# A two-layer recurrent block on one core: the next tile is normed channel by channel, B's rows go through memory, and the first round is reordered

## The reference, cut to what matters

```python
xn = _layernorm(x, axis=-1)
s = _L0_attn_ref(xn, ...)        # token-shift mixes, then the recurrence S = decay * S + k v^T
g = _silu(_L0_ffn_ref(xn, ...))  # gated, the two largest of every four hidden units are kept
x = x + s * g
xn = _layernorm(x, axis=-1)
s = _L1_attn_ref(xn, ...)        # 8 "heads" of 512 positions, chunked scan with B, C, X and decays
g = _silu(_L1_ffn_ref(xn, ...))
x = x + s * g
# inside _L1_attn_ref, a state per chunk:
states = jnp.einsum('znj,znjd,znjh->zndh', decay_states, Bc, Xc)
```

## Time and profile before

| | us |
|---|---|
| median of 3 runs (lowest, highest) | 761.48 (760.66, 761.60) |
| the profiled execution: its own time | 761.46 |
| its span in the profile | 759.7 |
| PE busy | 733.9 (97% of the span) |
| DVE busy | 505.5 (67%) |
| ACT busy | 326.0 (43%) |
| POOL busy | 76.6 (10%) |

### The profile page before, as it was taken

One profiled execution on the slowest core, in us unless ns is written; L12 is line 12 of the kernel. 1 busy time (PEld: TensorE's weight loads), 2 busy tenths in 40 slices (PEclk: granted clock), 3 DMA queues, 4 the chain that ended last, 5 costly groups with the idle time before them and its releaser, 6 DMA issues.

```text
span 759.7 us, 18508 instructions
## 1 busy us (share of the span) xinstructions
PE 733.9 (97%) x7316; PEld 601.5 (79%) x7316; DVE 505.5 (67%) x1177; ACT 326.0 (43%) x659; POOL 76.6 (10%) x85
## 2 busy tenths in 40 slices
PE   5897999999999999999999999999999999999997
PEld 3775778877888788886888868888788878888686
DVE  3886578736797367955778467884679736796143
ACT  1322575226632466214752157512664236631570
POOL 6201011101011011000110001100011101101020
PEclk9999999999999999999999999999999999999999
DMA  8800410005000150002400032001500014000320
GB/s 284 330 16 0 127 30 3 1 30 154 2 3 1 48 135 2 3 2 71 113 2 2 3 126 57 3 1 30 149 8 2 1 45 140 2 3 1 99 55 16
DMA packets 33938, 39.77 MB, mean 52 GB/s; under 512 B 20352, under 2 KB 27968, under 8 KB 32192
## 3 DMA queue, kind: packets, MB, share of 16 engines
q1 hardware_dynamic: 33856, 38.49, 16.9%
HBM read 32.12 MB, written 6.36 MB: 51 GB/s over the span
## 4 chain that ended last, share of the span: by engine, by line
PE 93%; DVE 4%; issue 1%; ACT 1%; DMA 0%; POOL 0%; DVEq 0%; SPq 0%; ACTq 0%; POOLq 0%
PE psum L1276 70%; PE psum L1378 4%; PE psum L1488 2%; PE psum L1473 2%; PE psum L1338 2%; PE psum L1349 1%; PE psum L1499 1%; PE psum L1707 1%; PE psum L1526 1%; PE psum L1304 1%; PE psum L1324 1%; PE psum L1361 1%; PE psum L1434 1%; PE psum L1634 1%; PE psum L1441 1%
## 5 line engine op out<-in xcount | busy, mean ns | idle before, releaser
L519 ACT ACTIVATE BC<-psum 64x256 f32<-64x256 f32 x128 | 81.2, 634 | 3.5 <-PE psum L1276 1.8
L1276 PE MATMUL psum<-xnT,sb_f_gate 128*128 128x256 f32 x248 | 62.6, 396 | 1.0 <-ACT xnT L532 0.8
L1276 PE MATMUL psum<-xn1T,sb_n_gate 128*128 128x256 f32 x256 | 61.4, 383 | 0.0
L1276 PE MATMUL psum<-xn1T,sb_n_up 128*128 128x256 f32 x256 | 60.5, 379 | 0.0
L1276 PE MATMUL psum<-xnT,sb_f_up 128*128 128x256 f32 x240 | 58.3, 385 | 0.0
L1276 PEld LDWEIGHTS psum<-xnT,sb_f_gate 128*128 128x128 f32 x248 | 46.2, 194 | 9.9 <-issue 1.7
L1276 PEld LDWEIGHTS psum<-xn1T,sb_n_up 128*128 128x128 f32 x256 | 48.6, 190 | 6.6
L1276 PEld LDWEIGHTS psum<-xn1T,sb_n_gate 128*128 128x128 f32 x256 | 47.3, 190 | 6.5
L867 DVE TENSOR_TENSOR kT<-kT,dec 128x256 f32<-128x256 f32 x56 | 25.7, 458 | 36.0 <-PE psum L1378 29.0
L1276 PE MATMUL psum<-sb_n_down,hidB 128*128 128x256 f32 x224 | 49.5, 379 | 0.0
L1276 PE MATMUL psum<-sb_f_down,hid 128*128 128x256 f32 x224 | 49.5, 379 | 0.0
(11 more groups left out here) (209 smaller groups left out, 1517.1 us busy)
## 6 DMA issues: line engine op xcount, KB each, us to landing
cs_row<-cs_dram SPq DMA_DIRECT2D x8, 1024.0 KB, 5.5
x_dram<-gate SPq DMA_DIRECT2D x8, 512.0 KB, 2.8
cs_half<-cs_dram SPq DMA_DIRECT2D x16, 256.0 KB, 6.4
hidB<-x_dram SPq DMA_DIRECT2D x8, 512.0 KB, 8.1
X<-in_x SPq DMA_DIRECT2D x9, 256.0 KB, 2.7
x<-in_x SPq DMA_DIRECT2D x8, 256.0 KB, 4.1
out_tokens<-thFB SPq DMA_DIRECT2D x8, 256.0 KB, 2.2
sb_w_rkvgo<-in_w_rkvgo SPq DMA_DIRECT2D x1, 1280.0 KB, 5.9
```

The lines of the kernel that those rows point to most:

```text
L519: ins = a_.activation(cols[:, par, 2 * pair:2 * pair + 2, :], src[64 * par:64 * par + 64, :, s, :], ACT.Identity)
L1276: ins = t_.matmul(ps(t, name)[first_row:first_row + rows, col:col + n], w, x, start=(k == 0), stop=(k == len(ws) - 1))
```

## The change

- The next tile is no longer normed by tokens and turned. A second copy of x is laid out on the host with channels on partitions (`x_turned`), and SP loads a tile of it (`XT`, 256 KB) with `X`. DVE's mean and POOL's result go into `token_stats` (128 x 2 x 2). SP stores that (2 KB) and loads it back to every partition (`rows`, 256 KB): step `token_rows`. `next_normed` then is two operations of 128x512 on `XT` (subtract, multiply) that write `xnT`, with the small carry of L975 between. `next_turned` on PE and `next_copied` on ACT are gone. Only tile 0 is still turned on PE.
- `cs16` and its transpose are gone. SP loads `cs_pos` (128 x 16, one float at a time) instead, behind `cs_row`, and POOL waits for `cs_row` alone. `end_args` moves forward on DVE to behind `level_step(2)`.
- `turned_B` is gone. DVE turns B in blocks of 32x32 into `B_turned` (two operations of 128x512, behind `level_step(2)` and `level_step(3)`), SP stores it in `b_dram` with four DMAs, in runs of 32 floats, and loads it back as `Brow` in runs of 64 floats, and `B_decayed` scales it in place. `states` waits for `B_ready`.
- On DVE some of the `sparse_*` steps move back to make room, and `decayed_scores(2)` moves ahead of `hidden_p(3)`. On ACT `end_exp` and the exponentials `L_exps` of layer 1 move forward, `sums_exp` behind them.
- First round: `rank_mix` stands between two halves of the gate product, `mixes` ahead of the up product, the decay weights are a group of their own ahead of the second pair of gate and up weights, and the projection weights follow. `next_normed` stands behind `states_0`.

The core of the diff:

```diff
+            def channels(tile):
+                return A["x_turned"][bass.ds(tile * P, P), :].rearrange("p (h t) -> p h t", h=CH)
+
+            def token_rows(a):
+                wait(rstd_ready, a.count(3, 2))
+                wait(rows_loaded, a.count(16, 16))
+                sp_.dma_start(A["row_dram"].rearrange("(q p two) -> p q two", q=NQ, p=P),
+                              token_stats[:, :, :]).then_inc(rows_stored, 16)
+                wait(rows_stored, a.count(16, 16))
+                sp_.dma_start(rows[:, :, :].rearrange("p t two -> p (t two)"),
+                              A["row_dram"].partition_broadcast(P)).then_inc(rows_loaded, 16)
...
-                    sp_.dma_start(cs16[:, :], cs_dram.rearrange("(c p) -> c p", p=P)).then_inc(cs_loaded, 16)
-                    sp_.dma_start(flat(cs_row), cs_dram.partition_broadcast(P)).then_inc(cs_loaded, 16)
+                    sp_.dma_start(flat(cs_row), cs_dram.partition_broadcast(P)).then_inc(cs_rows_loaded, 16)
+                    sp_.dma_start(cs_pos[:, :], cs_dram.rearrange("(c p) -> p c", p=P),
+                                  allow_slow_non_contiguous=True).then_inc(cs_loaded, 16)
...
+                    if a:
+                        token_rows(a)
+                    wait(B_rows, b.count(16, 16))
+                    wait(B_blocks, b.count(2, 2))
+                    to = b_dram.rearrange("(s n i e d) -> s e i n d", s=NQ, i=32, e=2, d=32)
+                    for s in range(NQ):
+                        for e in range(2):
+                            r = 64 * s + 32 * e
+                            sp_.dma_start(to[s, e], B_turned[r:r + 32, :].rearrange("p (n d) -> p n d", d=32)).then_inc(
+                                B_stored, 16)
+                    wait(B_stored, b.count(64, 64))
+                    sp_.dma_start(Brow.rearrange("p q c d -> p (q c) d"),
+                                  b_dram.rearrange("(c p d) -> p c d", p=P, d=SD)).then_inc(B_rows, 16)
...
-                    norm_apply(X, xn, a.count(3, 2), xn_ready)
-
-                    d.tensor_scalar(xnT[:, :, 0:1], xnT[:, :, T:T + 1], keep[:, bass.ds(a.next().at(), 1)], None,
-                                    ALU.mult).then_inc(carry_ready, 1)
+                    dve.wait_ge(rows_loaded, a.count(16, 32))
+                    dve.wait_ge(xT_loaded, a.count(16, 16))
+                    did(d.tensor_tensor(XT[:, :, :], XT[:, :, :], rows[:, :, 0].unsqueeze(1).to_broadcast([P, CH, T]),
+                                        ALU.subtract))
+                    did(d.tensor_scalar(xnT[:, :, 0:1], xnT[:, :, T:T + 1], keep[:, bass.ds(a.next().at(), 1)], None,
+                                        ALU.mult))
+                    after()
+                    d.tensor_tensor(xnT[:, :, 1:T + 1], XT[:, :, :], rows[:, :, 1].unsqueeze(1).to_broadcast([P, CH, T]),
+                                    ALU.mult).then_inc(xn_ready, 1)
...
+                def B_by_block(half):
+                    wait_freed(dve, b, "B0")
+                    dve.sem_inc(passed, 1)
+                    wait_freed(dve, b, "B1")
+                    n = slice(half * SEQ_T * SH // 2, (half + 1) * SEQ_T * SH // 2)
+                    d.transpose(B_turned[:, n], BC[:, 0, :, :].rearrange("p t h -> p (t h)")[:, n]).then_inc(B_blocks, 1)
...
                     level_step(a, 2)
+                    end_args()
+                    B_by_block(0)
+                    level_step(a, 3)
+                    B_by_block(1)
+                    level_step(a, 4)
                     sparse_compare(a, 0, 1)
                     sparse_compare(a, 0, 2)
-                    level_step(a, 3)
-                    sparse_sums()
-                    level_step(a, 4)
-                    sparse_rest()
                     level_step(a, 5)
                     gate_0()
                     last_update(a)
                     res_gate(0)
                     res_gate(1)
-                    end_args()
+                    sparse_count()
                     hidden_p(a, 2)
                     states_0()
                     B_decayed()
                     decayed_scores(0)
+                    decayed_scores(2)
                     hidden_p(a, 3)
-                    decayed_scores(2)
```

162 lines of the change are left out of this document (81 added, 81 removed), and 2 rows, old and new, of the table FILLS.

## The result

The changed kernel takes 759.57 us (median of 20 runs, 756.5 to 762.22), the kernel before beside it 761.10. The ratio is 0.9963, with a 95% interval from 0.9950 to 0.9976: faster by 0.37%, 2.8 us (the two medians themselves lie 1.5 apart). I had forecast 753.1, a gain of 8.4, three times what the ratio gives. The sign was right and the time lies in the range, but the median is 6.5 us above the forecast. The profiled execution has a time of its own of 760.17 and a span of 758.4.

The account below looks back on a forecast made before the run. PE's list was taken to bound the seven two-layer rounds. Span 759.7 - 1.9 (first round) - 7 x 0.98 + 0.4 (last round) = 751.3, plus 1.76 = 753.1 us; range 750 to 766, the forecast's own 750.7 to 756.2.

Parts of the forecast that it names:

- PE's list sets the round, and what leaves it comes back: Seven two-layer rounds: PE is busy 90.58 of 90.70 us; removing 1.08 of transposes gains 0.98 per round.
- First round: Time up to the end of the first round: net -1.9 us, between -1.2 and -2.6.
- the order: First round on PE: mixes ahead of the up product starts 1.93 earlier, and the shift of 1.9 stays.
- the late norm: First round on DVE: next_normed behind states_0 makes the second selection late, about 0.8 more wait for PE.
- the turning that goes: First round on PE: turning the next tile, a row of 1.06 overlapping the next by about 0.2, is gone.
- Last round: Last round: -0.64 again, but B's rows come late behind the load of X's rows, a wait of 1.04; +0.4.
- The transfers: New DMA transfers, all hidden in the rounds; B's store 6.25 and load 3.85, landing 1.9 ahead of 301.3.
- Late B: Rival: B's rows late at DVE's scaling, PE waiting at states and across; 778 at twice 18.8 ns, chance 0.18.
- the point from which it decides: B's round trip: run cost above which its rows come late, 26 ns a run; gain gone from 30.5 ns.
- PE's time turns into waits: Rival: new work on DVE or ACT makes PE wait, each round gains 0.2 instead of 0.98; 758.6, chance 0.14.
- the four slacks: Four places where PE could come to wait, with slacks of 0.1 to 0.5 us, cited for the waits rival.

Follow-up runs that it names:

- quad_before: Kernel before with 20 spare products at PE's start and 44 in the first round's wait, alternating between array quarters and two banks: 759.78 us, ratio 0.9964.
- quad_late: Changed kernel with only spare products added (20 at PE's start, 48 in the first round's wait), alternating between quarters and banks: 752.10 us, ratio 0.9864.
- quad_after: Changed kernel with the next tile's norm earlier in the first round and 20 and 48 spare products alternating between quarters and banks: 750.88 us, ratio 0.9853.
- pad16: Changed kernel with 16 increments of an unused semaphore ahead of everything on PE: 752.96 us, ratio 0.9879.
- quad_176: quad_after with 44 instead of 48 spare products in the middle, 16 instructions fewer: 757.25 us, ratio 0.9939.
- quad_last: quad_after with the states moved behind the last FFN pair on PE in the last round: 749.71 us, ratio 0.9837.
- spare_after: Changed kernel with 20 small unread products at PE's start and 48 in the first round's wait, all on the same quarter: 757.13 us, ratio 0.9912.
- old_first: Changed kernel with PE's first-round order of before (gate product whole, rank, up product, mixes): 760.38 us, ratio 0.9986.
- old_first16: pad16 with PE's first-round order of before (gate product whole, rank, up product, mixes): 757.24 us, ratio 0.9924.
- dear_store: norm_early16 with half of B's store done once more, ahead of the real one, into unread memory: 771.77 us, ratio 1.0117.
- norm_early16: pad16 with the next tile's norm back ahead of the first comparison in DVE's first round: 752.61 us, ratio 0.9845.
- dear_pool_later: dear_store with GpSimd's multiply of cs_half put behind DVE's scaling of B: 756.18 us, ratio 0.9928.

## Why the prediction was off, point by point

- **PE's list sets the round, and what leaves it comes back**: right. In quad_before and quad_late, with the blocks out of the way, the seven rounds differ by 7.61; forecast 7 x 0.98 = 6.9. Along one round (quad_after against quad_before, time from the steps) the scores come 0.61 earlier (forecast 0.64), the states 0.45 (a wait of about 0.16, forecast 0.1), the output product 0.90 (0.44 more, as forecast), the next steps 1.02.
- **The step that failed** is the unspoken one ahead of the sum: that 19 transposes fewer change nothing but their own time. They also move the program in its instruction blocks, and in the place where the changed kernel stands `within` breaks in every round. Cost in the seven rounds: 628.64 - 624.97 = 3.7 by pad16, 4.3 by quad_176; with the first round, where moving by 16 alone made the first steps 2.4 earlier, 6.4 (uncertain by 2.2) by the ratio of pad16 to the changed kernel. That is the size of what is missing. In the seven rounds the packets show what it is: PE waits for its instructions. No row of the trace of before showed such a break in a round; one in the first round did (a gap of 0.86 put down to issue, ahead of the matmuls of L1361), and I did not ask what it was.
- **First round**, forecast -1.9 net, made of -1.9 for the order, +0.8 for the late norm, -0.86 for the turning that goes. Order and norm were measured at 1.7 to 3.4 and 0.75 (the norm by PE's wait), both right within their uncertainty. The net at the first steps is -0.85 in quad_late, so some 1 us is missing, and +2.8 in the profiled run of the changed kernel, 4.7 off the forecast: in that execution more than the rounds lost. So this term failed as well: it carried PE's lead of 1.9 through to the end of the round. What differs there is the break of 0.70 and above all the granted clock: quad_late, quad_after, quad_last and quad_176 have the same PE program up to 50 us and yet start their last level at 46.34, 44.26, 44.89 and 44.98. Up to 34 us PE was busy alike in quad_late and quad_after (2.89 and 2.88 of the 4.00 from 30 to 34), and yet the stretch from 34 to 37 was granted 0.65 in the one and 1.00 in the other. The term for the first round needed a range of 2 to 3 us for the clock alone, not 1.4. Later in quad_after PE was busy for 1.34 of 3.00 at full clock, then came half clock:

```profile
44.00:47.00 3.00, 1.34 (x20) 0.99 (x20) 2.93 (x8) 2.27 (x5) 0.00 (x0) 1.00 0.00 0
47.00:50.00 3.00, 2.85 (x21) 2.38 (x22) 2.96 (x8) 0.10 (x1) 0.00 (x0) 0.56 0.28 89
```

- **Last round**, forecast +0.4 (-0.64 and a wait of 1.04): the mechanism right, the wait 1.1 to 2.0 in nine traces of kernels with the change and an unaltered store, and 0 in the profiled run of the changed kernel, where DVE had B's rows 24.4 after the steps and not 26.3 as in quad_after and quad_late. The rest grew by 0.96 in quad_late.
- **The transfers**: the store of 4096 runs of 128 bytes was forecast at 6.25 and took 6.5, the load at 3.85 and took 4.1; they landed 0.8 ahead of DVE's use, where I had 1.5 (299.4 against 300.9). The estimate worked out from the Trainium skill, "DMA: Bandwidth & Descriptors", section "Why small descriptors are slow" (store 1.7 shorter), did not hold. `cs_pos` took 5.4, not 1.8 to 2.4, and yet no one waited for it.
- **The rivals.** Late B did not happen in the rounds. But its price was wrong: the point from which it decides was near, and rows that are 0.8 to 2.0 late there bring 1.3 to 2.2 more through GpSimd. "PE's time turns into waits" named nearly the right time (758.6) by luck, with the wrong cause, since none of the four slacks it rests on was used up.
- **Sum again**, for the profiled executions: the seven rounds gave 3.4 instead of 6.9, the first round cost 2.8 instead of giving 1.9, the last gave 0.7 instead of costing 0.4. That is 7.1 less than forecast (760.17 against 753.1). It was a run of low clock. In the five runs at 0.995 the median is 757.6, so some 4.5 are missing, of which the late instructions in the seven rounds explain 3.7; the other 2 us up to the median of 759.57 go with the lower clock of the other runs, and that they all arise in the first round is not shown.

## What to carry to other kernels

When a change adds or removes instructions on an engine that is always busy, time a second copy with some idle instructions in front (here 16): if the two differ by more than the change, the placement was measured, not the change. Where a row "<-issue" stands at the same instruction in every round, compare its end with the instruction packets of the trace (here 1.2 to 1.7 us before), and where the row is the first of its group, look for the last producer first. When an operand moves from PSUM to SBUF, look at what GpSimd does beside that instruction.

## What the hardware showed that I had not expected

- 16 instructions more or less ahead of a loop: 6.4 us of 757 (quad_after, quad_176), 4.3 of it in the seven rounds. A program moved by 83 lost 1.7 us in each round.
- Such gaps end 1.2 to 1.7 us after the end of a 16 KB instruction packet (42 gaps in 17 traces).
- An increment of a semaphore on an otherwise idle PE takes 0.15 us (83 until 14.93, 173 until 28.65: 13.72 for 90).
- A 64x64 product with 32 columns takes 4.47/20 = 0.22 us when all use the same quarter of the array and one bank, at a granted clock of 1.00, and 1.29/20 = 0.06 when they alternate between quarters and two banks (rows of 40 at 2.7 us in spare_after and quad_after); in the middle of the first round 8.22/48 = 0.17, at a granted clock of 0.67, against 1.60/48 = 0.03. Quarters and banks were not told apart.
- Two multiplications of DVE with both inputs in SBUF took 3.32 instead of 1.16 beside a multiplication of GpSimd of 2.71; with one input in PSUM they took 1.15 beside it.
- Open: why the break in the first round (0.7 to 1.83 us in `before`, the changed kernel, pad16, old_first, old_first16, dear_store) did not come in norm_early16 and dear_pool_later, whose PE program is that of pad16 and dear_store. What the traces show is that a packet started at 31.48 and 31.78 in the two with the break and at 24.77 and 24.90 in the two without; what moved it, and what in a place makes a packet late, they do not show.
